# Four transformer blocks on one core: the order of work in the last stage is moved by a slot, and a bias goes to TensorE

## The reference

```
x = layernorm(x + L0_attn(x))   # causal attention, 16 heads of 64, over 1024 rows
x = layernorm(x + L0_ffn(x))    # 8 experts, each row goes to one
x = layernorm(x + L1_attn(x))   # per row: softmax over the 4 batch entries of squared distances
x = layernorm(x + L1_ffn(x))    # 16 experts of width 64, the two best weighted, and a shared one
```

## Time and profile before

| what | value |
|---|---|
| median of 3 runs | 1817.56 us |
| the runs | 1817.56, 1813.74, 1818.01 us |
| the profiled execution's own time | 1815.28 us |
| its span | 1813.4 us |
| busy: PE, DVE, ACT, POOL | 1602.4, 1035.1, 774.8, 580.4 us |
| first gather of the last stage | 1441.73 us |
| PE busy, granted clock, 1500 to 1520 us | 19.28 of 20, 0.97 |
| PE busy, granted clock, 1520 to 1540 us | 16.02 of 20, 0.91 |
| PE busy, granted clock, 1560 to 1580 us | 15.48 of 20, 0.83 |
| PE busy, granted clock, 1580 to 1600 us | 20.00 of 20, 1.00 |

### The profile page before, as it was taken

How to read it: one execution, slowest core, us unless ns; L and a number is a source line. 1 busy time by engine, 2 the same in 40 slices (tenths; PEclk the granted TensorE clock), 3 DMA queues, 4 the chain that set the end, 5 groups by cost and what they waited for, 6 DMA issues and landing times. The chain is left out here.

```text
span 1813.4 us, 28563 instructions
## 1 busy us (share of the span) xinstructions
PE 1602.4 (88%) x8973; PEld 756.6 (42%) x8974; DVE 1035.1 (57%) x2399; ACT 774.8 (43%) x1364; POOL 580.4 (32%) x581
## 2 busy tenths in 40 slices
PE   5799999999999999999999999995479638999998
PEld 2344444444444444444444444433356424333332
DVE  4455646555565555564665556656522257777765
ACT  2345444454454544545444444441034234444432
POOL 4253351533524425344253351511700141111000
PEclk8799999999999999999999999996589859999999
DMA  3502021120220202202022020002211100000000
GB/s 102 180 19 67 1 67 31 50 68 1 68 61 8 79 1 68 67 1 68 1 67 68 1 67 4 1 1 103 81 46 46 41 18 9 12 13 6 13 6 12
DMA packets 106706, 73.64 MB, mean 41 GB/s; under 512 B 5249, under 2 KB 100761, under 8 KB 106318
## 3 DMA queue, kind: packets, MB, share of 16 engines
q1 hardware_dynamic: 104526, 67.76, 12.2%
q0 software_dynamic: 2048, 4.20, 0.8%
HBM read 24.23 MB, written 47.71 MB: 40 GB/s over the span
## 5 line engine op out<-in xcount | busy, mean ns | idle before, releaser
L743 ACT ACTIVATE P<-S,keyb 128x386 f32<-128x386 f32 (+7 forms) x512 | 296.4, 630 | 389.4 <-PE S L539 386.2
L535 PE MATMUL S<-QT,KT 64*128 64x512 f32 (+5 forms) x1792 | 392.2, 492 | 9.4 <-DVE KT L881 7.3
L1061 POOL TENSOR_TENSOR rn<-nm,half 128x12 f32<-128x12 f32 x128 | 295.4, 2312 | 106.8 <-DVE nm L818 106.8
L1077 POOL TENSOR_SCALAR_AFFINE_SELECT P<-P 128x256 f32<-128x256 f32 (+1 forms) x256 | 156.1, 610 | 533.9 <-ACT P L743 533.9
L916 DVE TENSOR_TENSOR Psum<-Psum,P 128x1796 f32<-128x1796 f32 (+7 forms) x256 | 279.3, 1091 | 38.0 <-POOL P L1077 17.1
L559 PE MATMUL O<-P,V 128*64 128x512 f32 (+5 forms) x1536 | 255.4, 436 | 3.4 <-POOL P L1077 3.4
L535 PEld LDWEIGHTS S<-QT,KT 64*128 64x128 f32 (+1 forms) x1792 | 163.2, 183 | 202.2 <-issue 193.3
L539 PE MATMUL S<-GQ,GK 64*128 64x512 bf16 (+5 forms) x896 | 154.0, 309 | 0.0
L430 PE MATMUL W<-xT,wts 128*128 128x512 f32 x256 | 140.9, 644 | 9.8 <-DVE QT L877 7.2
L938 DVE TENSOR_TENSOR part<-W,rden 128x512 f32<-128x512 f32 x128 | 82.5, 686 | 92.7 <-PE W L607 92.7
L743 ACT ACTIVATE Psum<-S,keyb 128x1024 f32<-128x1024 f32 x64 | 67.8, 1110 | 137.2 <-PE S L539 69.8
(11 more groups left out here) (220 smaller groups left out, 2196.9 us busy)
## 6 DMA issues: line engine op xcount, KB each, us to landing
xg<-zero SPq DMA_DIRECT2D x16, 1216.0 KB, 7.2
yg<-zero SPq DMA_DIRECT2D x16, 1216.0 KB, 10.6
wts<-in_w_qkv SPq DMA_DIRECT2D x16, 384.0 KB, 3.8
gu<-in_gu SPq DMA_DIRECT2D x1, 2816.0 KB, 9.7
xb<-xg SPq DMA_DIRECT2D x40, 64.0 KB, 1.8
yg<-yb SPq DMA_DIRECT2D x40, 64.0 KB, 1.6
X<-in_x SPq DMA_DIRECT2D x4, 512.0 KB, 4.3
wo<-in_w_out SPq DMA_DIRECT2D x16, 128.0 KB, 2.3
```

The lines of the kernel that those rows point to most:

```text
L535: nc.tensor.matmul(S[hh][0:m, at + c:at + c + w], KT[d, r, p, jt * P:jt * P + m], QT[d, r, p, Q0[jt] + c:Q0[jt] + c + w], start=True, stop ...
L743: nc.scalar.activation(probs(p, jt)[0:m, hh, 0:n], S[hh][0:m, at:at + n], ACT.Exp, bias=keyb[0:m, r, (2 * p + hh) * NKT + jt:(2 * p + hh) ...
L1061: nc.gpsimd.tensor_tensor(rn[:, c, u], nm[:, c, u], powers, ALU.pow).then_inc(rn_ok, 1)
L1077: nc.gpsimd.affine_select(own, own, [[0, 2], [1, w]], ALU.is_ge, 0.0, base=NNULL if jt == 0 else 0, channel_multiplier=-1).then_inc(cut, 1)
```

## The change

- ACT, DVE and PE do the turn of the normed rows in slot 2 instead of 3, the router's matmul and logits in slot 3 instead of 4, both picks in slot 4 (were 6 and 7) and the weights in slot 5 (were at the head of 8).
- `weigh(u, 0)` and `weigh(u, 1)` stand behind `shared` of slots 6 and 7; they stood at the end of slot 5 and at the head of slot 6, next to each other.
- `arrive` goes from the head of slot 4 to the end of slot 3, and its root on POOL with it.
- The bias `out_b` was added on DVE (`own_rows`, one instruction of 128x512 in slot 1); now PE adds it in `form`, by four more matmuls with one row of ones against one row of the bias.
- On PE `down` of a slot now stands ahead of `share` in every slot (before in slot 0 alone).
- POOL issues the gathers of chunk 0, the first root, and then those of chunk 1; before both chunks' gathers came first.
- `x2` has two buffers, and ACT's waits in `rows_normed` go with it. The buffer `y1` is gone.

```diff
--- before.py
+++ after.py
@@ -1481,8 +1481,8 @@
             den = sb("den", [P, 2, NB * H1], F32, sc)
             o1 = sb("o1", [P, NB, D], F32, sc)
             ots1 = sb("ots1", [P, CH], F32, sc)
-            x2 = sb("x2", [P, NB, D], F32, sc)
-            y1 = sb("y1", [P, NB, D], F32, sc)
+            x2 = sb("x2", [P, 2, NB, D], F32, sc)
+            ones1 = sb("ones1", [1, P], F32, sc)
             y2 = sb("y2", [P, NB, D], F32, sc)
             sc1 = sb("sc1", [P, 4, NB, E1], F32, sc)
             eq = sb("eq1", [P, NB, E1], F32, sc)
@@ -1513,10 +1513,10 @@
             pick2 = s4("pick2")
             (init, x_ok, x2_mm, x2_ok, qv_mm, qv_ok, dif_ok, sqd_ok, dist_ok, wf_ok, den_ok, rden_ok, wn_ok, pr_ok, half_ok, o1_ok,
              o_mm, ots_ok, y_mm, yb_ok, x3_mm, x3_ok, r_mm, lg_ok, ex_ok, ex1_ok, sig_ok, rest_ok, num_ok, rd_ok, w_ok, part_ok,
-             w3_ok, c_mm, c_ok, yb_pre) = (
+             w3_ok, c_mm, c_ok) = (
                 s4(n + "4") for n in ("init x_ok x2_mm x2_ok qv_mm qv_ok dif_ok sqd_ok dist_ok wf_ok den_ok rden_ok wn_ok pr_ok half_ok "
                 "o1_ok o_mm ots_ok y_mm yb_ok x3_mm x3_ok r_mm lg_ok ex_ok ex1_ok sig_ok rest_ok num_ok rd_ok w_ok part_ok "
-                "w3_ok c_mm c_ok yb_pre").split())
+                "w3_ok c_mm c_ok").split())
             gu5, silu5, prod_ok, hid5_ok, dn5, ys5_ok, y5_t, x5_ok, m5, st_out = (
                 s4("gu5"), s4("silu5"), s4("prod_ok5"), s4("hid_ok5"), s4("dn5"), s4("ys_ok5"), s4("y_t5"),
                 s4("x_ok5"), s4("m5"), s4("st_out"))
@@ -1559,7 +1559,7 @@
                     wait_some(pe, c_ok, c - 1)
                     wait_some(pe, ots_ok, c)
                     for b in range(NB):
-                        last = nc.tensor.transpose(T[:, b, :], x2[:, b, :], idf[:])
+                        last = nc.tensor.transpose(T[:, b, :], x2[:, c % 2, b, :], idf[:])
                     last.then_inc(x2_mm, 1)
 
                 def project(c):
@@ -1586,7 +1586,8 @@
                     pe.wait_ge(qv_ok, c + 1)
                     wait_some(pe, lg_ok, c)
                     for b in range(NB):
-                        last = nc.tensor.matmul(Y1[:, b, :], ots1[:, b * P:(b + 1) * P], ow1[:], start=True, stop=True)
+                        nc.tensor.matmul(Y1[:, b, :], ots1[:, b * P:(b + 1) * P], ow1[:], start=True, stop=False)
+                        last = nc.tensor.matmul(Y1[:, b, :], ones1[:], ob1[0:1, :], start=False, stop=True)
                     last.then_inc(y_mm, 1)
 
                 def normed_turned(c):
@@ -1662,40 +1663,39 @@
                     k = NJ1 * (u - 2) + j
                     if live(u - 2):
                         gate_up(u - 2, j)
-                    if j == 0:
-                        if live(u - 1):
-                            form(u - 1)
-                        if live(u - 2):
-                            combine(u - 2)
-                    elif live(u - 2):
-                        share(u - 2, j)
+                    if j == 0 and live(u - 1):
+                        form(u - 1)
+                    if j == 0 and live(u - 2):
+                        combine(u - 2)
                     if 0 <= k - LAG < KS:
                         down(k - LAG)
                     if j == 0 and live(u):
                         rows_turned(u)
-                    if j == 0 and live(u - 2):
-                        share(u - 2, 0)
+                    if live(u - 2):
+                        share(u - 2, j)
                     if j == 1 and live(u):
                         project(u)
                     if j == 2 and live(u - 3):
                         last_turned(u - 3)
+                    if j == 2 and live(u - 1):
+                        normed_turned(u - 1)
                     if j == 3 and live(u - 1):
-                        normed_turned(u - 1)
-                    if j == 4 and live(u - 1):
                         route(u - 1)
                     if j == 8 and live(u):
                         sums_turned(u)
 
                 pe.wait_ge(ld_3, 16 * 7)
+                pe.wait_ge(init, 4)
                 periods(slot)
 
             @block.scalar
             def _(act):
                 def rows_normed(c):
 
-                    wait_some(act, yb_pre, c)
-                    wait_some(act, x2_mm, c)
-                    norm.scalar_apply(act, X[:, c], x2, n2(c))
+                    if c >= 2:
+                        act.wait_ge(yb_ok, c - 1)
+                        act.wait_ge(x2_mm, c - 1)
+                    norm.scalar_apply(act, X[:, c], x2[:, c % 2], n2(c))
 
                 def rows_home(c):
 
@@ -1791,12 +1791,12 @@
                         rows_home(u)
                     if j == 1 and live(u - 1):
                         norm2.scalar_apply(act, y2, X[:, u - 1], u - 1)
-                    if j == 3 and live(u - 1):
+                    if j == 2 and live(u - 1):
                         normed_home(u - 1)
+                    if j == 4 and live(u - 1):
+                        sigmoids(u - 1)
                     if j == 4 and live(u):
                         exponentials(u)
-                    if j == 4 and live(u - 1):
-                        sigmoids(u - 1)
                     if j == 8 and live(u):
                         sums_home(u)
 
@@ -1813,13 +1813,6 @@
                         dve.wait_ge(norm.done, n2(c - 1) + 1)
                     norm.vector_stats(dve, X[:, c], n2(c))
                     norm.vector_shift(n2(c))
-
-                def own_rows(c):
-
-                    dve.wait_ge(norm.done, n2(c) + 1)
-                    wait_some(dve, yb_ok, c)
-                    nc.vector.tensor_tensor(y1[:], x2[:], ob1[:].unsqueeze(1).broadcast_to([P, NB, D]),
-                                            ALU.add).then_inc(yb_pre, 1)
 
                 def differences(c):
 
@@ -1869,10 +1862,10 @@
 
                 def joined(c):
 
-                    dve.wait_ge(yb_pre, c + 1)
+                    dve.wait_ge(norm.done, n2(c) + 1)
                     dve.wait_ge(y_mm, c + 1)
                     wait_some(dve, norm2.done, c)
-                    nc.vector.tensor_tensor(y2[:], Y1, y1[:], ALU.add).then_inc(yb_ok, 1)
+                    nc.vector.tensor_tensor(y2[:], Y1, x2[:, c % 2], ALU.add).then_inc(yb_ok, 1)
                     dve.wait_ge(yb_ok, c + 1)
                     norm2.vector_stats(dve, y2, c)
                     norm2.vector_shift(c)
@@ -1949,18 +1942,10 @@
 
                 def slot(u, j):
 
-                    if j == 1 and live(u):
-                        own_rows(u)
                     if j == 2 and live(u):
                         differences(u)
                     if j == 3 and live(u):
                         distances(u)
-                    if j == 4 and live(u + 1):
-                        arrive(u + 1)
-                    if j == 6 and live(u):
-                        weigh(u, 1)
-                    if j == 8 and live(u - 1):
-                        weights(u - 1)
                     if live(u - 2):
                         gated(u - 2, j)
                     if j == 0 and live(u - 1):
@@ -1969,21 +1954,26 @@
                         shared(u - 2, j)
                     if j == 2 and live(u - 3):
                         ended(u - 3)
+                    if j == 3 and live(u - 1):
+                        logits(u - 1)
+                    if j == 3 and live(u + 1):
+                        arrive(u + 1)
                     if j == 4 and live(u - 1):
-                        logits(u - 1)
+                        pick_one(u - 1)
+                        pick_other(u - 1)
+                    if j == 5 and live(u - 1):
+                        weights(u - 1)
                     if j == 5 and live(u):
                         shares(u)
-                        weigh(u, 0)
-                    if j == 6 and live(u - 1):
-                        pick_one(u - 1)
-                    if j == 7 and live(u - 1):
-                        pick_other(u - 1)
+                    if j in (6, 7) and live(u):
+                        weigh(u, j - 6)
 
                 nc.vector.memset(wt[:], 0.0).then_inc(init, 1)
                 dve.wait_ge(init, 1)
                 nc.vector.memset(wt[:, 0, :, E1:NE1], 1.0).then_inc(init, 1)
                 dve.wait_ge(init, 2)
                 nc.vector.memset(wf[:], 1.0).then_inc(init, 1)
+                nc.vector.memset(ones1[:], 1.0).then_inc(init, 1)
                 periods(slot)
 
             @block.gpsimd
@@ -2001,15 +1991,16 @@
                         norm2.pool_shift(pool, u - 1)
                     if j == 2 and live(u - 3):
                         norm1.pool_shift(pool, n4(u - 3))
-                    if j == 4 and live(u + 1):
+                    if j == 3 and live(u + 1):
                         norm.pool_shift(pool, n2(u + 1))
+                        if u < 0:
+                            get_chunk(1)
                         if live(u + 3):
```

(1 more changed line is left out.)

## The result

The changed kernel takes 1840.01 us (median of 4 runs, 1835.88 to 1842.77) against 1816.31 before (4 runs): a ratio of 1.013, 95% interval 1.0106 to 1.0154. The forecast was 1817.2 with a range from 1806 to 1828. It is 24 us slower, and outside the range.

The account below looks back on a forecast made before the run. It took PE's slow slots, not the weighing, as the bound before `sums_turned`. Fill +9.0, first period -0.4, five steady periods -7.0 and drain +0.3 made +1.9 on 1815.3: 1817.2 us, range 1806 to 1828.

Parts of the forecast that it names:

- The bias on PE: Eight more passes in `form`, paid in full: +0.98 us a period at 2.4 GHz, 2.1 at 1.2 GHz.
- The rule on weight loads: PE's bias matmuls: load time goes by columns, not contraction, so one row of ones costs what 128 rows do.
- The steady period: Each of five periods: -2.4 us from DVE's new order, +1.0 for the bias, so -1.4; -7.0 in all.
- the DVE line: DVE's work from ended's first instruction to the second weighing's end in a steady period: 24.3 us.
- the three just-in-time waits: On DVE's line, logits, first pick and next silu could each wait 0 to 1 us; 0 to +6 over six periods.
- The fill: Start of the last stage, where no feed-forward work covers anything: +9.0 us in sum.
- the picks' part alone: Fill, period 1: picks and weights ahead of the weighings and `sums_turned`, +5.7 us in full, the largest single term.
- the 7.7 of the prediction: Sign in the fill: `sums_turned(1)` about 7.7 us later than in the kernel before.
- The first root: Fill, on POOL: the root no longer stands behind four gathers of chunk 1, -1.1 us.
- M behind Y: PE's order in the slots: M comes 0.9 us later and hid hardly waits; costed at nothing.
- the clock falls in the new stalls: Rival: PE's stalls drop the clock, `sums_turned` to `form` run slow, +2.7 us in six periods, 1833; chance 0.13.
- the bias terms: In `form`: +1.0 us a steady period, +2.1 for the fill's first `form`, +1.3 for its second.

Follow-up runs that it names:

- one condition: Kernel with the bias on DVE, with the weighings ahead of picks and weights again in period 1 alone: 1803.47 us.
- The two kernels that differ in nothing but the rows of the block: Kernel with the bias on DVE plus twelve matmuls ahead of `form`'s four: 1855.97 us with one row, 1831.23 with 128.

## Why the prediction was wrong

The step that failed is "The bias on PE", both as a term and in what hangs on it.

- *Its size.* I took eight more passes at `form`'s own 0.98 us and called the lower end 0 and the row the upper one. The nearest row was no upper bound: it was of 128 rows all through. A `form` with the bias costs 2.24 us more at the full clock, and at the lower one 5.8 instead of 2.1 (1471.66 to 1477.45), +3.7 for +2.1. With 128 rows the bias costs 0.90 a `form`, what the row said, and the kernel takes 1822.04, inside the range. The 0.2 us are paid by every matmul of the mixture, `form`'s own too. The range should have had an upper end above the row, since no row showed one-row work next to 128-row work.
- *What it does to the clock.* I had the clock fall in stalls only. It falls behind a `form` in which PE is busy, in four of the six steady periods. That costs Y and the turn behind `form` 1.4 us in the period shown. In the fill the clock comes up only at about 1519: the second `form` takes 5.6 us (1507.37 to 1513.00) where before it took 1.34, +4.3 for +1.3, and the first +3.7 for +2.1. These are 4.6 of the fill's 7 us too much; G, U and the turn behind the second are slow as well.
- *The rule on weight loads.* The Trainium skill ("TensorE: Matmul & The Clock Gate", LDWEIGHTS) has a load go by its columns, so that one row costs what 128 do. The trace agrees for the loads: half of the one-row ones take up to 184 ns, in the mixture too, and of `form`'s own in the same kernel up to 189. It says nothing of the matmuls, and these are what grew: their starts stand 0.41 apart in the mixture against 0.22 to 0.24 with 128 rows. The 81 ns a pass of its section on the back-to-back gap were no closer: float32 passes stood 0.11 apart at best.
- *The steady period* otherwise was right. Without the bias it was to change by -2.4; the four after the first changed by 39.1 - 41.0 = -1.9 in the mean, and by -2.8 in the two where the clock's fall cost nothing; the DVE line was to be 24.3 us and is 23.9; the three just-in-time waits cost nothing of note.
- *The fill* otherwise was right: -1.1 + 1.0 + 5.7 = +5.6 forecast without the bias, +4.6 measured, and the picks' part alone 5.7 against 5.8. In the changed kernel `sums_turned(1)` starts 63.6 us behind the first gather instead of 54.4, 9.2 later: the 7.7 of the prediction and 1.6 more of the first `form`. The first root came 8.71 us after the first gather instead of 9.77.
- *M behind Y*, forecast at nothing, is nothing that the runs can tell.
- *The clock's rule.* I weighed the rival "the clock falls in the new stalls" down by the Trainium skill's rule on single long gaps ("TensorE: Matmul & The Clock Gate", Part 1). The clock fell with no stall above 1.93 us, so these traces disagree with it as I applied it. In the kernel with the bias on DVE the price is 1.7 us in two of the four periods behind the first, not 2.7 in each.

The forecast without the bias terms would have been 1815.3 + 5.6 - 1.4 - 2.4 x 5 + 0.3 = 1807.8; the kernel with the bias on DVE measures 1809.4. That they are so close is in part luck: the fill came out 1.0 better than forecast, and the five periods after it 2.0 worse (194.0 us; 192.0 forecast), since the clock fell. The mechanism was right but for these falls and for one edit, which was priced by a neighbour that differed in the one respect that mattered.

What stays open: at how many rows between 1 and 128 the clock holds (only these two were tried), why it falls behind some `form`s and not behind all, whether the change of row count costs by the count or by the change alone, and whether M ahead of Y moves the clock's fall off the path by more than chance.

## What to carry to other kernels

A bias by a row of ones is not a free use of a busy TensorE: it cost 0.1 to 0.2 us at every change between one row and 128, and it can take the clock from the matmuls behind it. Where it must be on TensorE, give it all 128 rows (ones over 128; here 18 us faster than one row, but still 12.6 slower than on VectorE), or leave it on an engine that waits anyway, as VectorE did here for 0.7 us. And when work is reordered for the steady state, look at the fill, where the same order runs with nothing beside it: here it cost 5.8 us, and one condition gave them back.

## What was not expected of the hardware

- One-row matmuls in a block run at 0.12 us a pass, 128-row ones at 0.11; alternating, both kinds take 0.21 (0.36 at the lower clock, where plain `form` has 0.26).
- The clock fell to its lower level with PE busy in 100% of the stretch before, when that work was of one row (0.63 and 0.52 against 1.00 in the windows above). The two kernels that differ in nothing but the rows of the block are 24.7 us apart, part of it by the clock's fall behind the block.
- The clock also fell with no stall of PE above 1.93 us in the stretch before (0.58 over 1651 to 1655, behind one of 1.72, and 0.76 over 1619 to 1623, behind 1.71, 0.34 and 1.93), where in the kernel before it fell in one of 4.52.
